# Recurrent attention and a routed feed-forward layer: front part reordered, low halves of weight pieces made by adding transfers

## The reference

```python
q = layernorm(x); k = v = ctx                       # heads of 32
ig = concat(q, k, v) @ igate_kernel + igate_bias    # fg likewise
cs = cumsum(log_sigmoid(fg))
log_D[s, t] = cs[s] - cs[t] + ig[t]  where t <= s, else -inf
D = exp(log_D - rowmax(log_D)); C = (q @ k.T / sqrt(32)) * D
h = (C / (max(|rowsum(C)|, exp(-rowmax)) + 1e-6)) @ v
x = x + head_layernorm(h) * outnorm_weight
y = layernorm(x)                                    # routed layer
p = softmax of the 2 largest of y @ gate_w.T (8 experts)
h1, h2 = split(y @ w12[e].T)
x = x + sum over the 2 experts: p[e] * (silu(h1) * h2) @ w3[e].T
```

## Time and profile before

| | before |
|---|---|
| median of 3 runs | 682.49 us (681.91 to 683.64) |
| profiled execution: time | 679.7 us |
| profiled execution: span | 678.0 us |
| mean granted TensorE clock | 0.917 of full |
| TensorE busy | 570.1 us (84%) |
| VectorE busy | 469.3 us (69%) |
| ScalarE busy | 335.4 us (49%) |
| GpSimd busy | 310.0 us (46%) |

### The profile page before, as it was taken

One profiled execution on the slowest core, in us unless ns is written; L12 is line 12 of the kernel. 1 busy time (PEld: TensorE's weight loads), 2 busy tenths in 40 slices (PEclk: granted clock), 3 DMA queues, 4 the chain that ended last, 5 costly groups with the idle time before them and its releaser, 6 DMA issues.

```text
span 678.0 us, 14645 instructions
## 1 busy us (share of the span) xinstructions
PE 570.1 (84%) x3612; PEld 470.5 (69%) x3613; DVE 469.3 (69%) x987; ACT 335.4 (49%) x745; POOL 310.0 (46%) x316
## 2 busy tenths in 40 slices
PE   3867689989899864023999999999999999999993
PEld 1333567878778753012888888888888888888882
DVE  4572177888787887994676767677777767676763
ACT  2535255666667643201555555555555555555551
POOL 3312235556556550502355545454555555454532
PEclk9979578999999985555999999999999999999998
DMA  7763344455555433802233333333232333333332
GB/s 245 231 188 105 102 114 137 149 169 171 156 189 162 147 109 115 326 3 45 33 59 53 54 56 50 60 48 62 47 63 47 58 52 55 55 54 56 49 46 24
DMA packets 61148, 66.87 MB, mean 99 GB/s; under 512 B 12146, under 2 KB 55034, under 8 KB 61116
## 3 DMA queue, kind: packets, MB, share of 16 engines
q0 software_dynamic: 15552, 25.21, 20.4%
q1 hardware_dynamic: 36860, 32.88, 16.1%
q10 hardware_dynamic: 8704, 8.39, 3.5%
HBM read 43.24 MB, written 18.75 MB: 91 GB/s over the span
## 4 chain that ended last, share of the span: by engine, by line
issue 41%; DVE 19%; PE 13%; POOL 13%; DMA 8%; SPq 3%; ACT 2%; DVEq 0%; POOLq 0%; ACTq 0%
POOL xg L1127 8%; DMA out_rows<-ys,index 6%; PE bank L1246 5%; POOL out_rows L1136 4%; PE dots L1228 3%; DVE c L822 3%; DVE ohn L969 2%; DVE tot L863 2%; DVE ohp L968 2%; DVE st L701 2%; DVE mu L858 1%; PE dots L1179 1%; PE dots L1181 1%; DVE wden L859 1%; DVE wabs L857 1%
## 5 line engine op out<-in xcount | busy, mean ns | idle before, releaser
L1136 POOL DMA_INDIRECT out_rows<-ys,index x71 | 112.9, 1590 | 154.7 <-DVE ys L1021 143.5
L1027 DVE TENSOR_TENSOR w3l<-w,w3h 128x1024 fp32r<-128x1024 f32 x71 | 87.1, 1227 | 31.0 <-issue 30.0
L1127 POOL DMA_INDIRECT xg<-token_table,index x71 | 70.4, 992 | 51.8 <-DVE index L986 29.9
L667 ACT CAST w3h<-w 128x1024 fp32r x71 | 74.4, 1048 | 20.3 <-issue 20.3
L1246 PE MATMUL bank<-aug,c 128*128 128x99 f32 (+2 forms) x512 | 67.4, 288 | 15.7 <-DVE c L822 15.6
L1246 PEld LDWEIGHTS bank<-aug,c 128*128 128x128 f32 x512 | 63.6, 202 | 21.9 <-DVE c L822 20.1
L1368 PE MATMUL bank<-w3l,hth 128*128 128x256 f32 x284 | 76.5, 302 | 1.8 <-DVE w3l L1027 1.8
L1369 PE MATMUL bank<-w3h,hth 128*128 128x256 f32 x284 | 70.8, 282 | 0.0
L1021 DVE TENSOR_SCALAR ys<-bank,pc 128x256 f32<-128x256 f32 x71 | 34.3, 484 | 46.6 <-PE bank L1372 46.6
L1004 DVE TENSOR_TENSOR htl<-bank,hth 128x512 fp32r<-128x512 f32 x71 | 49.1, 691 | 25.1 <-ACT hth L657 25.1
L1340 PE MATMUL weighs<-w12l,xh 128*128 x144 | 62.0, 431 | 1.1 <-DVE xl L993 1.1
(11 more groups left out here) (165 smaller groups left out, 1246.9 us busy)
## 6 DMA issues: line engine op xcount, KB each, us to landing
wst<-in_w12T POOLq DMA_DIRECT2D x24, 256.0 KB, 3.6
aug<-in_ctxv SPq DMA_DIRECT2D x16, 264.0 KB, 3.7
w12h<-in_x SPq DMA_DIRECT2D x16, 256.0 KB, 2.9
w12l<-in_ctxT SPq DMA_DIRECT2D x16, 256.0 KB, 3.4
qbd<-w12h SPq DMA_DIRECT2D x64, 64.0 KB
x<-in_x SPq DMA_DIRECT2D x16, 256.0 KB, 2.8
out_rows<-x ACTq DMA_DIRECT2D x16, 256.0 KB, 2.1
token_table<-x2n ACTq DMA_DIRECT2D x16, 256.0 KB, 2.4
```

The costliest lines, as they stand in the source:

```text
L667: nc.scalar.copy(W3H[i][:], w3[:, bass.ds(e, 1)].rearrange("p a k d -> p (a k d)")).then_inc(w3h_ready, 1)
L1027: v.tensor_tensor(W3L[i][:], w3[:, bass.ds(e, 1)].rearrange("p a k d -> p (a k d)"), W3H[i][:].bitcast(F32), ALU.subtract).then_inc(w3l_re ...
L1127: q.indirect_dma_start(out=XG[x][:], out_offset=None, in_=table, in_offset=bass.IndirectOffsetOnAxis(ap=index[:, j:j + 1], axis=0)).then_i ...
L1136: q.indirect_dma_start(out=out, out_offset=bass.IndirectOffsetOnAxis(ap=index[:, j:j + 1], axis=0), in_=YS[o][:], in_offset=None, compute_ ...
```

## The change

Five parts.

1. Gates: ScalarE sends each batch's gates from `GS1` to a DRAM scratch `gate_scratch` with one transfer a round; SyncE reads the rows of four batches (`pair_gates(0)`, round 10), and of twelve after its loop, with two transfers each. The passes wait for these reads.
2. Front part: the mask constants are issued by GpSimd in rounds 2 and 4; queries, values and mask rows of batches 0 and 1 are loaded in or right behind SyncE's loop; the passes' steps are spread over rounds 9 to 15; the second pass begins in batch 0 instead of 1. `three_parts` takes a range of parts and does the same arithmetic.
3. Pieces 16 to 31: SyncE loads the raw piece into its place in `w12l`; ScalarE rounds it into `w12h` and writes the negated rounded piece into `wst` (called `minus`); GpSimd issues a transfer that adds `wst` to `w12l`. This happens two to three steps later than before.
4. Pieces 8 to 15, in the routing: the same, with the negated pieces in the room of `W3H` and `W3L`.
5. SyncE, ScalarE and GpSimd have all steps of the mixing written out. VectorE keeps its loop.

The diff is cut; the order in it is SyncE, ScalarE, VectorE, GpSimd, TensorE. Left out: semaphore names and counts, the definition of `MINUS`, `three_parts`, `mask_constants` (the same lines, issued on GpSimd), VectorE's second pass (from batch 1 to the end of batch 0).

```diff
+                rows_ = (AHEAD, REST)[part]
+                lo, hi = ((0, LEAD), (LEAD, B))[part]
+                for i in range(2):
+                    sp.wait_ge(gate_out[i], 8 * hi)
+                for k, dst in enumerate((gi, gf)):
+                    sp.dma_start(dst[rows_, :], gate_dram[lo:hi, k * NH:(k + 1) * NH, :]).then_inc(pair_in, 16)
             def pair_rows(part):
...
-            for b in range(B + 5):
...
+            for b in range(B + 1):
...
-                if b in (9, 11):
-                    mask_constants((b - 9) // 2)
-                if 0 <= old:
-                    sp.wait_ge(gates_ready, old + 1)
-                    at = (old - LEAD) % B * NH
-                    for k, dst in enumerate((gi, gf)):
-                        sp.dma_start(dst[at:at + NH, :], GS1[old % 2][k * NH:(k + 1) * NH, :]
-                                     ).then_inc(gate_out[old % 2], 16)
-                if b == B:
-                    pair_rows(0)
+                if b == 10:
+                    pair_gates(0)
+                if b in (12, 13):
                     sp.wait_ge(zeroed, 1)
-                    load_queries(0, 0)
-                if b == B + 1:
-                    sp.wait_ge(parts_out, 16 * (1 + PARTS))
-                    load_gates(0, 0)
+                    load_queries(b - 12, b - 12)
+                if b in (14, 15):
+                    load_values(b - 14, b - 14)
+            pair_rows(0)
+            sp.wait_ge(parts_out, 16 * (1 + PARTS))
+            for b in range(2):
+                load_gates(b, b)
+            pair_gates(1)
...
-                if has(b, 0):
-                    wait(sp, s_ready, 2 * NG * (b - 1))
-                    if not isinstance(b, int) or b >= 1:
-                        load_gates(b, i)
-                        load_queries(b, i)
+                if has(b, 0) and not (isinstance(b, int) and b < 2):
+                    sp.wait_ge(s_ready, 2 * NG * (b - 1))
+                    load_gates(b, i)
+                    load_queries(b, i)
+                if has(b, 2):
+                    sp.wait_ge(s_ready, 2 * NG * (b - 1))
+                    sp.dma_start(kept(flat_l, b - 2).rearrange("p k s -> p (k s)"),
+                                 w12T[:, bass.ds((b - 2 + KEPT) * HID, HID)]).then_inc(raw_in[i], 16)
...
-                if has(b, 0):
-                    wait(sp, pv_group, NC * (b - 1))
-                    sp.dma_start(AUG[i][:].rearrange("p c h d -> p c (h d)"), ctxv_t[b]).then_inc(inv3[i], 16)
-                    sp.dma_start(KN[i][:], ctx_t[b, :, 0, :]).then_inc(inv3[i], 16)
+                if has(b, 0) and not (isinstance(b, int) and b < 2):
+                    sp.wait_ge(pv_group, NC * (b - 1))
+                    load_values(b, i)
+                if isinstance(b, int) and b == LEAD - 2:
+                    pair_rows(1)
                 if isinstance(b, int) and b == LEAD - 1:
-                    pair_rows(1)
                     sp.wait_ge(parts_out, 32 * (1 + PARTS))
                     sp.wait_ge(zero_out, 64)
-            mixing(sp, step)
+            for b in range(B + 3):
...
@@ -455,7 +463,9 @@
             for n in range(KEPT // 2):
                 at = (KEPT // 2 + n) * HID
                 sp.dma_start(room(flat_l, KEPT // 2 + n, HID), w12T[:, at:at + HID]).then_inc(late_in[n], 16)
-            sp.wait_ge(w_lo, W2)
+            sp.wait_ge(w_lo, W1)
+            for i in range(2):
+                sp.wait_ge(added[i], 16 * (B // 2))
             for e in range(NE):
                 sp.dma_start(w3[:, e], w3T[:, e * KH * E:(e + 1) * KH * E].rearrange(
...
                     act.wait_ge(gates_psum, a_ + 1)
-                    wait(act, gate_out[i], 16 * (a_ - i))
+                    wait(act, gate_out[i], 8 * (a_ - i))
                     nc.scalar.copy(GS1[i][:], bank[2 + i][0:2 * NH, 0:S]).then_inc(gates_ready, 1)
+                if has(b, 3):
+                    a_ = b - 3
+                    act.wait_ge(gates_ready, a_ + 1)
+                    act.dma_start(gate_dram[a_], GS1[o][:]).then_inc(gate_out[o], 16)
                 if b % 2 and has(b, 2):
                     n = (b - 3) // 2
...
-                if b == 8:
+                if b == 9:
                     act.wait_ge(late_consts, 16 * N_LATE)
                     forget(0)
                 if b == 11:
-                    gate_parts(0, 0, 2)
+                    gate_parts(0, 0, 1)
+                if b == 12:
                     decays(0)
-                if b == 12:
+                if b == 13:
+                    gate_parts(0, 1, 2)
+                if b == 14:
                     gate_parts(0, 2, 3)
...
+                if isinstance(b, int) and b == 0:
+                    forget(1)
...
-                if isinstance(b, int) and b == 0:
-                    forget(1)
...
-                if has(b, 0):
-                    act.wait_ge(inter_ready, b + 1)
-                    high(b + KEPT, wst[i][:], IN1 + 8 * (b - i) + 16, wst_in[i])
+                if has(b, 2):
+                    act.wait_ge(inter_ready, b - 1)
+                    high(b - 2 + KEPT, kept(flat_l, b - 2).rearrange("p k s -> p (k s)"), 8 * (b - 2 - i) + 16,
+                         raw_in[i])
+                    act.wait_ge(w_hi, W1 + b - 1)
+                    act.wait_ge(w_lo, W1)
+                    wait(act, added[i], 8 * (b - 2 - i))
+                    nc.scalar.mul(minus[i][:], kept(flat_h, b - 2).rearrange("p k s -> p (k s)"), -1.0
+                                  ).then_inc(minus_ready, 1)
...
-            mixing(act, step)
+            for b in range(B + 3):
...
             for n in range(KEPT // 2):
                 high(KEPT // 2 + n, room(flat_l, KEPT // 2 + n, HID), 16, late_in[n])
+                act.wait_ge(w_hi, W2 + n + 1)
+                nc.scalar.mul(MINUS[n], room(flat_h, KEPT // 2 + n, HID), -1.0).then_inc(minus_hi, 1)
...
-                if b == 8:
+                if b == 10:
                     preactivation(0)
-                if b == 10:
+                if b == 11:
                     maxima(0)
-                if b == 11:
-                    three_parts(dve, v, negM, AHEAD, m_parts, 0)
-                if b == 14:
+                if b == 12:
+                    three_parts(dve, v, negM, AHEAD, m_parts, 0, 0, 2)
+                if b == 13:
+                    three_parts(dve, v, negM, AHEAD, m_parts, 0, 2, 3)
+                if b == 15:
                     columns(0, bank[4])
...
+                if b in (2, 4):
+                    mask_constants(b // 2 - 1)
...
-                if has(b, 0):
-                    load_w(b + KEPT, i, W1 - 1 + b)
-                if has(b, 1):
-                    low(b - 1 + KEPT, wst[o][:], W1 + b)
+                if has(b, 3):
+                    pool.wait_ge(minus_ready, b - 2)
+                    q.dma_start(flat_l[:, bass.ds((b - 3 + KEPT) * HID, HID)], minus[o][:],
+                                accum_op=ALU.add).then_inc(added[o], 16)
...
-            mixing(pool, step)
+            for b in range(B + 3):
...
             for n in range(KEPT // 2):
-                low(KEPT // 2 + n, room(flat_l, KEPT // 2 + n, HID), W2 + n + 1)
+                pool.wait_ge(minus_hi, n + 1)
+                q.dma_start(flat_l[:, (W1 + n) * HID:(W1 + n + 1) * HID], MINUS[n].bitcast(F32), accum_op=ALU.add).then_inc(late_lo, 16)
...
-                if b == 13:
+                if b == 14:
```

More of the change, by code:

```diff
@@ L225, in build @@
         W3L = [sb(f"w3l{i}", [P, KH * E], F32R, on=f) for i in range(2)]
+        MINUS = [t[:, n * HID:(n + 1) * HID] for t in W3H + W3L for n in range(2)]
         YS = [sb(f"ys{i}", [P, E], on=f) for i in range(2)]
@@ L322, in loaded, with three_parts @@
             return 16 * n * ((b - i) // 2 + 1) if isinstance(b, int) else (b - i) * (8 * n) + 16 * n
[L324 to L327 removed]
+        def three_parts(eng, ops, src, rows_, counter, base_, lo, hi):
+            for q in range(lo, hi):
+                from_ = src[rows_, :] if q == 0 else rest[rows_, 0, q - 1, :]
+                ops.tensor_copy(parts[rows_, 0, q, :], from_).then_inc(counter, 1)
                 if q + 1 < PARTS:
                     eng.wait_ge(counter, base_ + 2 * q + 1)
[L330 removed]
+                    ops.tensor_tensor(rest[rows_, 0, q, :], from_, parts[rows_, 0, q, :],
                                       ALU.subtract).then_inc(counter, 1)
                     eng.wait_ge(counter, base_ + 2 * q + 2)
[L333 removed]
         block = stack.enter_context(nc.Block())
@@ L522, in forget @@
                 rows_ = (AHEAD, REST)[part]
-                for i in range(2):
-                    act.wait_ge(gate_out[i], 16 * (LEAD, B)[part])
+                act.wait_ge(pair_in, 32 * (part + 1))
                 nc.scalar.activation(fa[rows_, :], gf[rows_, :], ACT.Abs, bias=fb[rows_, 0:1]).then_inc(abs_ready, 1)
@@ L551, in _ @@
             act.wait_ge(eps_set, 1)
-            for b in range(B + 2):
+            for b in range(B + 3):
```

(19 more changed lines are left out.)

43 lines of the change are left out of this document (21 added, 22 removed).

## The result

The changed kernel takes 654.09 us (median of 4 runs, 652.82 to 656.97) against 682.20 of the kernel before beside it: a ratio of 0.959, interval 0.955 to 0.963. Timed again later in six runs it took 654.75 us (653.01 to 656.73), ratio 0.961 (0.958 to 0.963). The forecast was 656.5, range 644 to 672. The profiled execution took 654.9 us, its span is 653.1.

A forecast was written before the change was run, and what follows sets the result against it. No engine was taken as full: in the mixing TensorE idles 0.93 us a batch for VectorE. Stage gains 1 + 7 + 5.8 + 7.5 + 0.7 + 4 = 26 us off 682.5 gave 656.5, range 644 to 672.

The forecast's parts named there:

- Front part: Start to the last gates: smaller stalls and fuller clock, less ScalarE's issues and mask transfers; +1 us, between -6 and +6.
- the term of 4.3 us: Front part: ScalarE's one transfer issue per batch loses 0.27 us x 16 = 4.3 us, between 0 and 8.
- rival B: Front part: each gate copy waits for the transfer issued one round before, 6.4 us lost, total 663; chance 0.10.
- Gap: Last gates to first values: 10.65 us falls to 3.6 with two batches' loads ahead; +7 us, 2 less if mask rows late.
- the clock penalty goes with the holes: Batches 0 to 4 of the mixing: the mean clock of 0.81 recovers, part of a +5.8 us gain, between 2 and 9.
- by this row an issue holds VectorE off as well: Mixing batch: GpSimd's transfer issue also delays VectorE's 1.68 us product, so 1.2 us of it is saved.
- the floor is 9.45: Mixing batches 5 to 15: TensorE's busy time of 9.45 us is the least a batch can take; pace forecast 9.7.
- Tail and routing: Last batches and routing, up to the first gather: no GpSimd subtractions blocking VectorE; +0.7 and +4 us, the latter between 1 and 6.4.
- A: Mixing keeps its pace: none of the 7.5 us and half of the 5.8 gained, total 667; chance 0.15.
- C: Mixing: adding transfers hold back the keys behind them, 31 us lost, total 695; chance 0.04.
- D: Routing: VectorE's one-hot products hold off GpSimd's adding issues, at worst 4.7 us later, total 661; chance 0.05.
- E: The reordering does not do what it says: first scores still wait for loads, total 665; chance 0.04.

The follow-up runs named there:

- second profile: Nothing changed: the changed kernel profiled again in its later timing; 654.75 us (653.01 to 656.73), 0.961 of the kernel before.
- sub_route: Changed kernel with the last eight pieces, in the routing, subtracted by GpSimd again; 661.77 us, 0.973 of the kernel before.
- sub_mix: Changed kernel with pieces 16 to 31 subtracted by GpSimd again, their loads staying with SyncE; 658.32 us, 0.967 of the kernel before.
- before_swap: Kernel before, with GpSimd's subtraction put ahead of its issue of the next load in each mixing batch; 676.33 us (one run).
- sub_keys: Changed kernel with the edits of both sub_mix and keys_first; 657.82 us (one run).
- keys_again: The same kernel as keys_first, timed again; 653.23 us, 0.958 of the kernel before.
- keys_first: Changed kernel with SyncE loading values and keys ahead of the raw piece and x in each mixing step; 652.99 us, 0.960 of the kernel before.
- masks_late: Changed kernel with the mask constants issued by GpSimd in rounds 6 and 8 instead of 2 and 4; 657.1 us, 0.963 of the kernel before.

## Why the prediction was right, point by point

**The total** was right, 654.1 against 656.5: 24.9 us between the two spans (23.1 to the second profile) and 28.1 between the medians, where the sum said 26. Several of its terms were wrong and offset each other, so a total as near as this is in part luck.

**Front part** (+1.5, and -1.8 in the second profile; forecast +1). Within the range, but with wrong terms. Where no copy waits for a transfer, two gate copies take 5.44 us (27.69 to 33.13), 2.72 each, not 2.87: the issue on ScalarE costs 0.08 us a batch over the 2.64 of before (23.76 to 29.04), not 0.27, so the term of 4.3 us was 1.3. What I had left to rival B came on top in most profiles, the waits for the copy's transfer. The early masks cost about 4 us (TensorE idle 2.96 before 21.12, then a granted clock of 0.54 from 22 to 25), not 1.0. The hole behind the first gate pass shrank to 3.82, for which I had 3.1. That the clock would be near full from 38 us on is false: it is 0.64 from 45 to 49 in this profile, so part of those 2.5 us was not gained.

**Gap** (+6.6; forecast +7). Right: 4.04 us, where I had said "within 4 us", and 4.24 in the second profile. What lies in it is a gate copy at 64.69, scores, exponents, and the values at 68.66.

**Batches 0 to 4** (+3.7; forecast +5.8). The step that failed is "the clock penalty goes with the holes": from 96 to 104 us the granted clock is 0.58 once more. Ahead of it stand a VectorE product of 1.96 us at 90.21 and waits of TensorE, 1.42 us for the block matrix of the queries and 0.78 for VectorE. sub_route, which has the same mixing, has the same product (1.97) and the same waits (1.42 and 0.79), and keeps the full clock (1.00 over all of these batches). The window of the changed kernel, then that of sub_route (columns as in the earlier trace rows):

```profile
96.00:104.00 8.00, 7.65 (x38) 6.51 (x38) 4.80 (x12) 5.49 (x15) 4.64 (x8) 0.58 0.82 246
```

```profile
96.00:104.00 8.00, 6.22 (x51) 5.39 (x52) 6.46 (x15) 6.36 (x17) 3.26 (x6) 1.00 0.83 246
```

Batches 0 to 4 of sub_route took 41.54 us, 3.0 less than here and 6.7 less than before. So the lower clock accounts for the 2.1 us that were missing, and none of these waits brings it down by itself; what does stays open.

**Batches 4 to 15** (9.89; forecast 9.7). Here the reasoning failed, not only a size. First, "by this row an issue holds VectorE off as well" is wrong: 0.17 us within an issue. Second, the gain was put down to the subtraction's 1.27 us. sub_mix keeps the subtraction and has the whole gain (0.53 a batch); 0.34 of it is the place of the load's 0.56 us issue ahead of the subtraction (before_swap), the rest was not taken apart. The subtraction's own 0.4 to 0.5 (sub_keys against keys_again and keys_first) was taken back, because the residual sum and the product with the decay then met VectorE's remaining products. Third, "the floor is 9.45" took TensorE's busy time in one batch of before as the least; batches in which it waits for nothing take 9.32. The later keys, which I feared through the DMA share, came (landing in 4.1 us instead of 3.5 in the median, DMA share 0.76 instead of 0.53 in the middle batches), but they cost TensorE 2.0 us in all of the middle (1.1 in the second profile). My sign of being wrong, that the product with cols still waits for the keys and TensorE for it, came true in kind, and is small.

**Tail and routing** (+8.4; forecast 4.7). The mechanism was right, the terms too small. The tail gave some 2.5 (8.4 less sub_route's 5.9; sub_mix loses 2.7 there), not 0.7. The routing gave 5.9 (sub_route), not 4: my upper end of 6.4 was near, and the allowance of 2.4 for eight issues hindering VectorE was for an effect that no row shows. The issues themselves take 0.86, not 0.56.

**The rivals.** A, no gain of pace: refuted, 5.4 to 6.4 us came of the 7.5. B, gate transfers bind: its mechanism is real. The first profile has one such wait, of 0.57 us, but the second has waits of 1.18, 1.87, 2.02 and 0.68 us, 5.8 in all, and masks_late 1.3 to 3.3 us at five copies; I gave it 0.10 and it happens in seven of ten profiles, at a price in the last gates of 1.7 us rather than 6.4. C, slower: nothing of it. D, issues starve: not seen; the trap of "SBUF: two separate sides" in the Trainium skill's "SBUF — State Buffer" does not show beside these one-hot operations, each issue being 0.86 us. Whether it has a part in the late landings (8.5 to 18.0 us, at a DMA share of 1.03) is not shown. E: no.

## What to carry to other kernels

When an operation takes far longer than its size, look for what ends with it on GpSimd, and then what GpSimd does next: with the one blocker removed the following product can meet VectorE instead, so here the gain went with the change of the sum over VectorE's four two-input products, not with the one product that had been longest. The order on GpSimd's queue (transfer issues of 0.6 to 0.9 us ahead of or behind a product) decides which of VectorE's operations is hit. A wait that is large in sum (50 us for the keys) can be worth little (1.1 and 1.5 us between the medians): ask what stands behind it in the engine that sets the end.

## What the runs showed of the hardware that I had not expected

- An accumulating transfer of 128x512 f32 within SBUF costs GpSimd 0.84 us of issue, a plain load 0.56 us; it lands in 4.4 us in the median in the mixing, and in 8.5 to 18.0 us in the routing beside the other loads. With only 16 columns the issue is the same, 0.84.
- VectorE operations with one input can be long as well beside GpSimd: the integer steps of 64 columns took 1.19 us beside GpSimd's subtractions and 0.20 without. Which resource that is stays open.
- When two two-input products of VectorE and GpSimd overlap, both stretch, not only VectorE's: 1.75 us instead of 0.68 and 0.92 instead of 0.63.
- A small transfer issued by ScalarE costs 0.08 us of its round, at 0.31 to 0.41 us of issue, where no copy waits: nearly all of an issue lies beside the copy ahead of it. Waiting for the landing is dearer: up to 2.0 us at one copy in the changed kernel, 3.3 in masks_late.
- With the same mixing and the same waits of TensorE ahead, the granted clock from 96 to 104 us was 0.58 in one kernel and 1.00 in the other.
